# Jobs before the second pair of scores, late sums, and three buffers for the weights in a TensorE-bound attention and FFN kernel

## What is computed

```python
xn = _layernorm(x, axis=-1)
s = attn(xn)            # softmax(rope(Q) rope(K)^T / 4, causal) V, then Wo
g = _silu(ffn(xn))      # ffn: fwht(x*SU)/64 -> silu(x Wg) * (x Wu) -> fwht -> Wd
x = x + s * g
```

## Time and profile before

| | us |
|---|---|
| median of 3 runs | 898.69 (897.32 to 899.49) |
| the profiled execution | 898.44 |
| its span, first to last instruction | 896.7 |
| TensorE busy | 796.7 |
| VectorE busy | 561.8 |
| ScalarE busy | 498.4 |
| GpSimd busy | 431.9 |

### The profile page before, as it was taken

One profiled execution on the slowest core, in us unless ns is written; L12 is line 12 of the kernel. 1 busy time (PEld: TensorE's weight loads), 2 busy tenths in 40 slices (PEclk: granted clock), 3 DMA queues, 4 the chain that ended last, 5 costly groups with the idle time before them and its releaser, 6 DMA issues.

```text
span 896.7 us, 14216 instructions
## 1 busy us (share of the span) xinstructions
PE 796.7 (89%) x5120; PEld 482.2 (54%) x5120; DVE 561.8 (63%) x999; ACT 498.4 (56%) x682; POOL 431.9 (48%) x476
## 2 busy tenths in 40 slices
PE   3767899887989999999989999999999999999951
PEld 2545777766755555555555545555555555554521
DVE  3997355325676776666757676776777767676401
ACT  3434443532456667566665666766667556766640
POOL 3776573554641646125562355525447324834534
PEclk9998999988999999999989999999999999999976
DMA  7445233525402212313233533433434233351243
GB/s 273 149 152 169 71 121 114 181 78 195 111 1 90 77 48 77 99 61 85 81 101 110 150 84 107 99 112 96 134 103 120 84 96 100 105 135 57 98 145 117
DMA packets 62421, 98.27 MB, mean 110 GB/s; under 512 B 10512, under 2 KB 27536, under 8 KB 62352
## 3 DMA queue, kind: packets, MB, share of 16 engines
q1 hardware_dynamic: 60768, 95.53, 34.9%
q10 hardware_dynamic: 1584, 1.84, 0.6%
HBM read 59.06 MB, written 38.01 MB: 108 GB/s over the span
## 4 chain that ended last, share of the span: by engine, by line
PE 55%; DVE 9%; ACT 4%; DMA 3%; issue 2%; POOL 2%; SPq 0%; POOLq 0%; ACTq 0%
PE ps L280 15%; PE ps L1229 11%; PE ps L1213 9%; PE ps L290 8%; PE ps L1190 7%; DVE ps L1425 4%; DVE mx L1430 2%; PE ps L1263 2%; ACT a_sb L300 1%; PE ps L1201 1%; ACT probs L1330 1%; DVE a_sb L321 1%; DMA scr_inv<-inverse 1%; ACT x_ffn L1342 1%; PE ps L1248 1%
## 5 line engine op out<-in xcount | busy, mean ns | idle before, releaser
L1330 ACT ACTIVATE probs<-ps 128x1024 f32<-128x1024 f32 (+1 forms) x320 | 292.2, 941 | 110.2 <-PE ps L1213 108.4
L1430 DVE TENSOR_REDUCE mx<-ps 128x4 f32<-128x512 f32 (+1 forms) x192 | 215.9, 1134 | 104.8 <-PE ps L1190 60.2
L1093 POOL TENSOR_SCALAR_AFFINE_SELECT probs<-probs 128x256 f32<-128x256 f32 (+1 forms) x192 | 92.2, 484 | 272.7 <-ACT probs L1330 272.1
L1425 DVE CUSTOM_DVE_ANT_0 ps<-ps,tri 128x384 f32<-128x384 f32 (+1 forms) x256 | 154.2, 646 | 35.7 <-PE ps L1190 35.6
L1229 PE MATMUL ps<-probs,v_ones 128*32 128x512 f32 (+3 forms) x1536 | 157.0, 496 | 2.7 <-POOL probs L1093 2.2
L1213 PE MATMUL ps<-q_s,k_s 64*128 64x512 f32 (+3 forms) x768 | 148.7, 413 | 9.7 <-DVE mx L1425 4.2
L1213 PEld LDWEIGHTS ps<-q_s,k_s 64*128 64x128 f32 x768 | 67.2, 184 | 157.1 <-issue 76.7
L1190 PE MATMUL ps<-k_s,q_s 48*128 48x512 f32 (+3 forms) x768 | 122.4, 368 | 9.4 <-PEq L371 5.2
L280 PE MATMUL ps<-xh,wug_hi 128*128 128x512 f32 x256 | 111.3, 435 | 17.1 <-DVE a_sb L321 16.4
L335 POOL TENSOR_TENSOR a_sb<-a_sb,u_sb 128x512 f32<-128x512 f32 x64 | 82.3, 1288 | 68.9 <-ACT u_sb L308 68.9
L280 PE MATMUL ps<-xh,wug_lo 128*128 128x512 f32 x256 | 102.7, 401 | 0.0
(11 more groups left out here) (116 smaller groups left out, 1064.6 us busy)
## 6 DMA issues: line engine op xcount, KB each, us to landing
scr_qk<-kinds SPq DMA_DIRECT2D x64, 256.0 KB, 2.3
q_s<-scr_qk SPq DMA_DIRECT2D x64, 128.0 KB, 2.9
k_s<-scr_qk SPq DMA_DIRECT2D x64, 128.0 KB, 3.0
scr_heads<-o_raw SPq DMA_DIRECT2D x32, 256.0 KB, 2.1
x_sb<-in_x SPq DMA_DIRECT2D x8, 512.0 KB, 4.4
scr_v<-v_st SPq DMA_DIRECT2D x16, 256.0 KB, 2.8
scr_gate<-y_sb SPq DMA_DIRECT2D x16, 256.0 KB, 2.8
q_s<-scr_qk SPq DMA_DIRECT2D x64, 64.0 KB, 3.0
```

What stands on the lines that cost most here:

```text
L1093: pool.affine_select(out=part, in_=part, compare_op=ALU.is_ge, fill=0.0, base=0, pattern=pattern, channel_multiplier=-1).then_inc(cut, 1)
L1330: act.activation(probs[:, n % 2, p, :, 0:w], ps[:, bank:bank + 2, 0:w], ACT.Exp, scale=SCALE).then_inc(exp_ok, 1)
L1425: last = dve.tensor_tensor_reduce(part_of, part_of, sh.tri[:, CH - w:CH], 1.0, LOWEST, ALU.add, ALU.max, mx[:, v % 2, kind, h, i % TPC:i % ...
L1430: last = dve.tensor_reduce(out[:, :, pairs[0]:pairs[0] + n], ps[:, banks[0]:banks[0] + 2, 0:n * w].rearrange('p e (x k) -> p e x k', x=n), ...
```

## The change

The FFN jobs move into the first gap. In the second gap now stand tiles 1 and 2 and the sums of step s-1, which were in the first; scores (s+1, 0) stay the border between the gaps. ScalarE does its jobs before exponential (s+1, 0) instead of behind it, and copies of heads and high parts behind that exponential. VectorE reads tile 0, does its jobs, and reads tiles 1, 2 and 3. The scores of s+1 both take pair B; the tiles take B, C, A, C. `probs` has three buffers instead of two (`NPROB`), and an exponential waits for the sums three steps back.

```diff
-    for what, banks in zip(s0 + s1[:1], (PAIR_A, PAIR_C, PAIR_A)):
+    for what, banks in zip(s0 + s1, (PAIR_A, PAIR_C, PAIR_B, PAIR_B)):
         pair_of[what] = banks
-    pair_of.update(zip(tiles, (PAIR_B, PAIR_B, PAIR_C, PAIR_C) if now else (PAIR_B, PAIR_C, PAIR_B, PAIR_C)))
-    pair_of.update((what, PAIR_B) for what in s1[1:])
-    for what in s0[:1] + tiles[:1] + s0[1:] + s1[:1] + tiles[1:3 if now else 2]:
+    pair_of.update(zip(tiles, (PAIR_B, PAIR_C, PAIR_A, PAIR_C) if now else (PAIR_B, PAIR_C, PAIR_B, PAIR_C)))
+    for what in s0[:1] + tiles[:1] + s0[1:] + (tiles[1:2] if not now else []):
         give(what, pair_of[what])
...
     if now:
-        for what in s1[1:] + tiles[3:]:
+        for what in s1[:1] + tiles[1:3] + s1[1:] + tiles[3:]:
             give(what, pair_of[what])
...
+    NPROB = 3
...
-        probs = sb('probs', [P, 2, NPAIR, 2, CH])
+        probs = sb('probs', [P, NPROB, NPAIR, 2, CH])
...
                 if now:
                     scores(u, s, 1)
-                    if s:
-                        weigh(u, s - 1)
-                    elif u:
-                        weigh(u - 1, NS - 1)
-                if now:
-                    scores(u, s + 1, 0)
-                for t in tiles[1:3 if now else 2]:
-                    max_tile(*t)
+                elif tiles:
+                    max_tile(*tiles[1])
                 for m, j in enumerate(jobs_at[z]):
...
                     job(j)
                 if now:
+                    scores(u, s + 1, 0)
+                    for t in tiles[1:3]:
+                        max_tile(*t)
+                    if s:
+                        weigh(u, s - 1)
+                    elif u:
+                        weigh(u - 1, NS - 1)
                     scores(u, s + 1, 1)
...
-                if n >= 2:
-                    act.wait_ge(pv_ok, n - 1)
+                if n >= NPROB:
+                    act.wait_ge(pv_ok, n - NPROB + 1)
...
                 if now:
                     for p in range(NPAIR):
                         exponentials(*now, p)
+                if 0 <= z - 1 < NR:
+                    for j in ups(z - 1):
+                        hidden_high(*j[1:])
+                for j in jobs_at[z]:
+                    job(j)
+                if now:
+                    exponentials(now[0], now[1] + 1, 0)
                 if r == 0 and u >= 1:
                     take_heads(u - 1, 1)
                 if at(z, 'high') is not None:
                     high_part(at(z, 'high'))
-                if 0 <= z - 1 < NR:
-                    for j in ups(z - 1):
-                        hidden_high(*j[1:])
-                if now:
-                    exponentials(now[0], now[1] + 1, 0)
-                for j in jobs_at[z]:
-                    job(j)
                 if now:
                     exponentials(now[0], now[1] + 1, 1)
...
-                ahead = 3 if steps_at(z) else 2
+                ahead = 1 if steps_at(z) else 2
```

More of the change, by code:

```diff
@@ L1087, in cut_ahead @@
                 if n == 1:
-                    part = probs[:, nth_step(u, s) % 2, p, :, 0:P]
+                    part = probs[:, nth_step(u, s) % NPROB, p, :, 0:P]
                     pattern = [[0, 2], [1, P]]
                 else:
-                    part = probs[:, nth_step(u, s) % 2, p].rearrange('p e (x n) -> p e x n', x=n)[:, :, :, 0:P]
+                    part = probs[:, nth_step(u, s) % NPROB, p].rearrange('p e (x n) -> p e x n', x=n)[:, :, :, 0:P]
                     pattern = [[0, 2], [0, n], [1, P]]
@@ L1229, in weigh @@
                         last = pe.matmul(ps[VW * h:VW * (h + 1), PV_BANK, q0:CH], v_ones[u % 2][:, j, h, :],
-                                         probs[:, nth_step(u, s) % 2, h // 2, h % 2, col:col + w],
+                                         probs[:, nth_step(u, s) % NPROB, h // 2, h % 2, col:col + w],
                                          start=j == 0, stop=j == TPC * (c + 1) - 1)
@@ L1326, in exponentials @@
                 act.wait_ge(scored, NPAIR * n + p + 1)
-                if n >= 2:
-                    act.wait_ge(pv_ok, n - 1)
+                if n >= NPROB:
+                    act.wait_ge(pv_ok, n - NPROB + 1)
                 bank = pair_of['scores', u, s, p][0]
-                act.activation(probs[:, n % 2, p, :, 0:w], ps[:, bank:bank + 2, 0:w], ACT.Exp,
+                act.activation(probs[:, n % NPROB, p, :, 0:w], ps[:, bank:bank + 2, 0:w], ACT.Exp,
                                scale=SCALE).then_inc(exp_ok, 1)
```

## The result

The changed kernel takes **928.38 us** (median of four runs, 927.43 to 930.1) against 898.78 for the kernel before beside it: ratio 1.0329, 95% interval 1.0311 to 1.0348. The forecast was 916, with a range of 902 to 928: the side and the mechanism are right, the size is 12 us too small, just beyond the range's end.

The account below looks back on a forecast made before the run. TensorE, 89% busy, was taken as the bound, with VectorE's order setting its waits. 898.4 + 17 (41 us of waits for 24) + 2.5 at the end = 917.9, taken as 916; range 902 to 928.

Parts of the forecast that it names:

- Rival B: Faster, 890 us: TensorE's path behind tile 1 hides the bunched reads even when a gate starts them late; chance 0.17.
- Rival D: No difference, 899 us: gates lose at tile 2 what they lost at the next scores, old and new waits cancel; chance 0.07.
- Rival C: Much slower, 931 us: the clock falls, with five more stretches like round 30's at 3 us each; chance 0.10.
- The old waits: Some 24 us of waits in the 71 ordinary rounds of the kernel before, all taken as removed and counted anew.
- Step (3): Three tiles read in one bunch: next second scores late by 0.55 (r=4), 0.5 (r=1), 0.3 (r=0), 0 (r=2, r=3) us.
- Step (4): Last job's reader: second-place gate loses at least 0.95 us at tile 2, up 0.2; single gates and downs delay the bunch.
- The last step: From the sum of 917.9 down to 916 us, as longer waits give VectorE time that single sums do not see.
- (5): Four rounds with x transposes: 11 us of waits again, so 0, with 3 us either way.
- (1): Third buffer for the weights: with two, exponentials of step s+1 would wait for late sums; gain by itself 0.
- (2): Jobs behind the first three pieces: waits of tiles 1 and 3 and scores of s+1 go, most of 24 us.
- (6): Rounds 82 to 84: both score pairs of s+1 share pair B, so ScalarE waits twice a round: +2.5 us.
- (7): ScalarE's heads copy and high part move behind an exponential, GpSimd's low parts wait for one, SyncE's rows not later: 0.

Follow-up runs that it names:

- experiment 4: Changed kernel with VectorE reading only the last 128 columns of each tile part, and the sums of step s-1 between tiles 1 and 2: 874.71 us.
- experiment 7: Changed kernel with tile 1 and its read behind the first large job, and the sums of step s-1 ahead of tile 2: 941.67 us.
- experiment 1: Changed kernel with the sums of step s-1 between tile 1 and tile 2 instead of behind tile 2: 927.84 us.
- experiment 8: Kernel before with three weight buffers instead of two: 898.95 us; changed kernel with two instead of three: 1013.1 us.
- Experiment 9: Changed kernel with the sums of step s-1 ahead of the first scores of s+1 instead of behind tile 2: 969.96 us.

## Why the prediction was right or wrong

**Mechanism and side: right.** The second place's gate holds tile 2 (0.9 us in the waits), three reads follow in a row, and the second scores come 0.06 us behind the last; Rival B (TensorE's path hides the bunch) and Rival D (old and new cancel) fall with rounds 39 and 54, and Rival C with the clock, 0.99 in the rounds of both kernels. The Trainium skill's rule that was weighed there ("TensorE: Matmul & The Clock Gate", "A second HAM failure mode: psum-queue depth-cycling") did not bite at this size of wait: 44 of the 75 rounds now hold one of 0.3 to 1.6 us at tile 2 (all but one at most 1.1), and the granted clock of the rounds is what it was.

**The old waits: right.** The prediction had 24 us in the 71 ordinary rounds. Counted from each round's last job to the next round's first, with 0.25 us a round taken off for what is there without any late bank, they were 24.

**The new ones: 51 us, not 41.** The same count, by what the last large job is; "forecast" is the prediction's sum by kinds, sorted anew:

| last large job | rounds | forecast | measured |
|---|---|---|---|
| gate as second job | 17 | 17.6 | 21.7 |
| up as second job | 19 | 7.2 | 10.8 |
| down | 14 | 4.3 | 5.0 |
| down that ends its sum | 8 | 6.2 | 7.0 |
| single gate | 4 | 3.5 | 4.0 |
| single up | 4 | 0.5 | 0.9 |
| piece | 5 | 2.1 | 1.8 |

51 less 24 is 27, where the forecast had 17; the transposing rounds take 1 off (below), so the count ends 1 us under the stretch's 27.1. The steps that failed are two terms, both in r=0 and r=2, which hold 7 of the 10 us (the other 3 are spread over the kinds, a few tenths or less a round):
- *Step (3), "r=0 ... the heads' copy ...: 0.3 in all".* The copy's wait is right (0.32 at the sums of s), but it does not stand beside the wait at tile 2: in round 55 TensorE loses 0.27 at tile 2, 0.11 at the sums behind it, and then 0.32 at the copy. With an up last r=0 costs 0.74 where 0.3 was taken, with a gate 1.54 where 0.95 was. (Four rounds each: 4 us.)
- *Step (4), "0.2, seen only where (3) costs nothing".* An up in second place makes tile 2 late by 0.27 to 0.37 in every kind of round, and each wait there is followed by 0.11 at the sums. In r=2 this is 0.49 for 0.2, and for a gate 1.22 for 0.95. (Five rounds each: 3 us.)

For r=4 and r=1, where VectorE's bunch sets the time, the terms stand: 0.64 and 0.50 for an up last against 0.55 and 0.5, 1.29 and 1.2 for a gate against 1.2 and 1.15. So what failed is how terms were joined: for each kind of round I took one chain, the later one, as if TensorE's waits on the way were inside it. They are where VectorE sets the end, and add up where TensorE does.

**The last step, "the longer waits now give VectorE time that the single sums do not see, so I take 916"**, had the wrong sign; without it the sum was 917.9. No row had shown the gain that it took for granted.

**(5) Transposing rounds, the same either way: right**, 9.7 us after, 10.8 before. **(1) Third buffer: right**, 0 by itself; that without it the change would cost 114 us, the prediction had only as "would wait". **(2) Tile 1 and the scores of s+1 wait for nothing: right** for scores (s+1, 1) and tile 1 (9.2 us gone), *wrong for tile 3*: it is late by 7.8 us (5.4 before), since behind a down that ends its sum or a single gate the read of tile 1 that frees its banks now comes behind that job's readers (0.54 us in such rounds). Its size lay in (4), under "single gates and downs". **(6) The end**: +3.4 for +2.5; half of it is the shared pair B, the cause of the rest stays open. **(7)**: the heads' copy was not free, as above; 2.2 us stand in the waits for it.

**What the change lost by.** By the runs: of 27 us, some 5 are the length of the bunched reads and some 10 the length of the job's readers (tanh, product, scaling); by medians 4 and 7. What remains hangs on tile 2 taking the pair that the second job leaves: with short reads in both orders, moving tile 2 behind the sums turns 22 us above the old order into 10 below it (experiment 4). These shares are differences at one point; since the chains are parallel they are not what repairing one would bring (2 us for tile 2's wait, 23 for the reads, 55 for both). No run leaves the order alone and gives tile 2 another pair of banks.

## To carry to other kernels

When a bank's reader and the queue of that reader both stand between two matmul groups, there are two chains, and a table of waits shows only the one that TensorE meets first: removing a 29 us line brought 2 us here, since the other ended at nearly the same time. Work out for each such place both the latest release and TensorE's own path with all waits on it added up, and say which one sets the end before terms are joined. Before an experiment that shortens a thing in the new kernel is read as the cost of the change, make the same edit in the old one: 23 us shrank to 5 that way.

## What the runs showed of the hardware

**A change of tiling costs TensorE some 0.1 us.** In experiment 7 the matmuls are the same, and the shortest spacings grow by 16.7 us in 75 rounds. With the 3 us of experiment 1 taken off, that is 0.11 for each of two more changes in 63 rounds, an estimate. **A stop just ahead of such a change costs 0.1 more**: behind its wait tile 2's pair of matmuls in round 39 takes 0.43 to the sums (540.93 to 541.36), and in the 16 rounds where a full tile 2 does not wait it is 0.32 to 0.33.

**The clock bears waits of 1 us in a quarter of the rounds, but not in nearly all.** With two buffers (experiment 8) TensorE waits up to 1.2 us at scores (s+1, 1) in nearly every round, and the granted clock falls twelve times in the rounds, to 0.5 of full speed (1.2 of 2.4 GHz), where before and after have one fall; its mean over the span is 0.937 against 0.965 (0.937 to 0.952 in its four runs). One such stretch:

```profile
495.00:500.00 5.00, 3.69 (x14) 2.63 (x11) 1.38 (x2) 1.65 (x4) 2.26 (x4) 0.52 0.15 31
```

This is what the Trainium skill describes ("TensorE: Matmul & The Clock Gate", "A second HAM failure mode: psum-queue depth-cycling"), idling between matmul groups while banks are cycled, and here the trace agrees; for the changed kernel, with 30 us of such waits instead of 120 (tile 2's 30 and 90 more), it does not. Experiment 9 lies between: at scores (s+1, 1) it waits as often, 66 times by TensorE's list against 65, but 0.7 us at most against 1.2, and it has one fall, as before. Its waits are also fewer in sum (33.3 us against 71.9 there), so whether the length of a wait or the sum decides, no run here tells.
